# Routed blocks of a mixture-of-experts layer: register reads moved to the head of a step, TensorE's loop turned by one product

## What is computed

```python
shared_out = _silu_and_mul(xf @ shared_w1.T) @ shared_w2.T
probs = jax.nn.softmax(logits.astype(jnp.float32), axis=-1)
routing_weights, selected = jax.lax.top_k(probs, TOP_K)          # 6 of 16
combine = zeros.at[jnp.arange(T)[:, None], selected].add(routing_weights)
gate_up = jnp.einsum('th,eoh->teo', xf, w1)                       # 512 -> 2 * 352
act = _silu_and_mul(gate_up)
moe_out = jnp.einsum('te,tei,ehi->th', combine, act, w2)          # 352 -> 512
```

## Time and profile before

| | us |
|---|---|
| median of 3 runs | 2193.07 |
| lowest and highest run | 2185.72, 2206.43 |
| the profiled execution, its own time | 2193.82 |
| its span, first to last instruction | 2192.1 |
| TensorE busy in the span | 2042.5 (93%) |
| VectorE, ScalarE, GpSimd busy | 1085.6, 949.4, 1039.2 |
| TensorE's granted clock over the span | 0.975 of full speed |

### The profile page before, as it was taken

How to read it: one execution, slowest core, us unless ns; L and a number is a source line. 1 busy time by engine, 2 the same in 40 slices (tenths; PEclk the granted TensorE clock), 3 DMA queues, 4 the chain that set the end, 5 groups by cost and what they waited for, 6 DMA issues and landing times.

```text
span 2192.1 us, 41896 instructions
## 1 busy us (share of the span) xinstructions
PE 2042.5 (93%) x12188; PEld 1828.2 (83%) x12189; DVE 1085.6 (50%) x2355; ACT 949.4 (43%) x2127; POOL 1039.2 (47%) x1070
## 2 busy tenths in 40 slices
PE   3999999999999999999968997899999999999997
PEld 2888888888888888888857886889999999988886
DVE  5555545555667676767545546333333333332322
ACT  4555545554565565656534410233333333333322
POOL 3444434442444445454546206367643223588864
PEclk9999999999999999999878998999999999999999
DMA  8877767777777776756324226467544333489898
GB/s 311 291 247 250 245 227 242 257 240 278 270 260 260 291 266 238 275 205 231 113 84 166 87 86 218 153 215 252 198 139 143 119 118 120 153 201 201 191 189 211
DMA packets 189240, 451.53 MB, mean 206 GB/s; under 512 B 21696, under 2 KB 21952, under 8 KB 189120
## 3 DMA queue, kind: packets, MB, share of 16 engines
q1 hardware_dynamic: 135648, 339.73, 45.3%
q0 software_dynamic: 21504, 51.13, 9.9%
q10 hardware_dynamic: 31968, 59.12, 8.4%
HBM read 276.41 MB, written 173.48 MB: 205 GB/s over the span
## 4 chain that ended last, share of the span: by engine, by line
PE 81%; issue 4%; DMA 3%; DVE 3%; ACT 3%; POOL 3%; SPq 0%; ACTq 0%; POOLq 0%
PE bank L1170 19%; PE bank L1046 13%; PE bank L1180 10%; PE bank L1094 8%; PE bank L1064 6%; PE bank L178 5%; PE bank L730 5%; PE bank L1112 3%; PE bank L740 3%; PE bank L1076 3%; PE bank L747 2%; POOL ex L1353 1%; PE bank L1104 1%; PE bank L478 1%; DMA xT<-xT_ffn 1%
## 5 line engine op out<-in xcount | busy, mean ns | idle before, releaser
L1170 PE MATMUL bank<-w_hi,xT 128*128 x1776 | 477.4, 331 | 19.3 <-issue 17.5
L1046 PE MATMUL bank<-w_hi,xT 128*128 128x512 f32 x1024 | 355.9, 409 | 13.8 <-DMA xT<-xT_att 9.3
L1170 PEld LDWEIGHTS bank<-w_hi,xT 128*128 128x128 f32 x1776 | 316.0, 188 | 42.2 <-issue 40.3
L1339 POOL TENSOR_TENSOR rr<-rr,expo 128x4 f32<-128x4 f32 x128 | 128.9, 1007 | 417.7 <-DVE rr L1456 417.7
L757 DVE TENSOR_TENSOR hT<-bank,hT 128x384 fp32r<-128x384 f32 x143 | 79.7, 557 | 439.2 <-ACT hT L754 439.2
L1170 PE MATMUL bank<-w_lo,xT 128*128 x888 | 286.6, 323 | 0.0
L1046 PEld LDWEIGHTS bank<-w_hi,xT 128*128 128x128 f32 x1024 | 197.8, 193 | 55.3 <-issue 13.2
L1180 PE MATMUL bank<-w_hi,hT 128*128 x666 | 229.5, 398 | 2.1 <-DVE hT L757 2.1
L754 ACT ACTIVATE hT<-bank 128x384 fp32r<-128x384 f32 x143 | 70.2, 491 | 341.8 <-PE bank L747 341.4
L1064 PE MATMUL bank<-w_hi,xT 128*128 128x256 f32 x1024 | 213.6, 292 | 0.0
L1094 PE MATMUL bank<-w_hi,oT 128*128 128x512 f32 x512 | 193.5, 419 | 20.0 <-DVE qkT L1451 18.3
(11 more groups left out here) (228 smaller groups left out, 4535.8 us busy)
## 6 DMA issues: line engine op xcount, KB each, us to landing
xT<-xT_att SPq DMA_DIRECT2D x128, 512.0 KB, 4.1
w_hi<-w_split SPq DMA_DIRECT2D x64, 512.0 KB, 6.6
w_lo<-w_split SPq DMA_DIRECT2D x64, 512.0 KB, 7.4
xg<-blank SPq DMA_DIRECT2D x111, 264.0 KB, 4.4
yg<-blank SPq DMA_DIRECT2D x111, 256.0 KB, 4.6
raw<-in_weights SPq DMA_DIRECT2D x88, 272.0 KB, 3.0
w_split<-w_hi SPq DMA_DIRECT2D x64, 272.0 KB, 3.4
w_split<-w_lo SPq DMA_DIRECT2D x64, 272.0 KB, 3.4
```

Source lines behind the costliest of these rows:

```text
L1046: last = pe.matmul(bank[par][:, :], xT[:, par, a, c * P:(c + 1) * P], w_hl[w][:, fw, c * 512:(c + 1) * 512], start=n == 0, stop=n == 11)
L1170: last = pe.matmul(out_[:, 0:I], xT[:, par, a, c * P:(c + 1) * P], flat(w_hl[w])[:, bass.ds(at + (c * 2 * I + half_ * I), I)], start=n == ...
L1339: pool.tensor_tensor(rr[:, :], rr[:, :], expo[:, :], ALU.pow).then_inc(pw_done, 1)
```

## The change

Three things change, all in the routed blocks. On TensorE a step now begins with all its reads, `w_at` of block i, `w_need` of block i, and `w_at` of block i-2, and then does the second product of block i-2 before the gate half of block i. The last product of the old step i-1 has become the first of the new step i, and the loop has its own shape (`blocks`) with one more step at the end; the order of all products and transpositions is as before. On ScalarE a step begins with the reads of `r_need` and `w_col`. From step ROUNDS_BY = 57 on, ScalarE doesn't read `r_need` but waits for all 6 rounds by a constant; its loop is split in two there. No other engine's program changes.

```diff
--- before.py
+++ after.py
@@ -916,6 +916,7 @@
             step(NBLK - 1, 0, True, False, False, True)
             step(NBLK, 1, False, False, False, True)
 
+        ROUNDS_BY = 3 * B + 9
         ROUTE_AT = 20
         COUNT_AT = 21
 
@@ -1183,15 +1184,21 @@
                             n += 1
                     last.then_inc(yF_done, 1)
 
-                def block_step(i, par, front, nxt, load, back):
+                def block_step(i, par, front, nxt, mid, back):
                     if front:
                         at = pe.value_load(w_at[0:1, bass.ds(i, 1)], min_val=0, max_val=WCOLS)
                         need = pe.value_load(w_need[0:1, bass.ds(i, 1)], min_val=HB, max_val=E * HB)
+                    if back:
+                        last_at = pe.value_load(w_at[0:1, bass.ds(i - 2, 1)], min_val=0, max_val=WCOLS)
+                        pe.wait_ge(hT_hi, NSH + i - 1)
+                        pe.wait_ge(hT_lo, NSH + i - 1)
+                        second_at(last_at, YF[par])
+                    if front:
                         pe.wait_ge(w_ready, need)
                         pe.wait_ge(xs_hi, i + 1)
                         pe.wait_ge(xs_lo, i + 1)
                         first_at(par, at, 0, GATE[par], g_done)
-                    if back:
+                    if mid:
                         pe.wait_ge(hid_done, NSH + i)
                         hidden_transposes(pe, HT_)
                     if nxt:
@@ -1199,17 +1206,23 @@
                         transposed(1 - par, trS)
                     if front:
                         first_at(par, at, 1, UP[par], u_done)
-                    if back:
-                        last_at = pe.value_load(w_at[0:1, bass.ds(i - 1, 1)], min_val=0, max_val=WCOLS)
-                        pe.wait_ge(hT_hi, NSH + i)
-                        pe.wait_ge(hT_lo, NSH + i)
-                        second_at(last_at, YF[1 - par])
+
+                def blocks(step):
+
+                    step(0, 0, True, True, False, False)
+                    step(1, 1, True, True, True, False)
+                    with pe.Fori(2, NBLK - 2, 2) as i:
+                        step(i, 0, True, True, True, True)
+                        step(pe.snap(i + 1), 1, True, True, True, True)
+                    step(NBLK - 1, 0, True, False, True, True)
+                    step(NBLK, 1, False, False, True, True)
+                    step(NBLK + 1, 0, False, False, False, True)
 
                 pe.wait_ge(table_out, 3)
                 pe.wait_ge(added, NSH)
                 pe.wait_ge(x_in[0], 16)
                 transposed(0, trS)
-                sparse(pe, block_step)
+                blocks(block_step)
 
             @block.scalar
             def _(act):
@@ -1289,18 +1302,26 @@
                         act.activation(pr[:, :, :], lg[:, :, :], ACT.Exp).then_inc(ex16, 1)
                 shared(act, shared_step)
 
-                def load(i, par):
-                    need = act.value_load(r_need[0:1, bass.ds(i, 1)], min_val=1, max_val=TOPK)
+                def load(i, par, need):
                     act.wait_ge(rounds, need)
                     act.dma_start(xin[par], xg[bass.ds(i * P, P), :]).then_inc(x_in[par], 16)
 
-                def split_hi(i, par):
+                def rounds_for(i):
+                    return act.value_load(r_need[0:1, bass.ds(i, 1)], min_val=1, max_val=TOPK)
+
+                def weight_at(i):
+                    return act.value_load(w_col[0:1, bass.ds(i, 1)], min_val=D, max_val=DW - 1)
+
+                def split_hi(i, par, col):
                     act.activation(xT[:, par, 0, :], TX_[:, :], ACT.Copy).then_inc(xs_hi, 1)
-                    col = act.value_load(w_col[0:1, bass.ds(i, 1)], min_val=D, max_val=DW - 1)
                     act.activation(cc[:, par:par + 1], xin[par][:, bass.ds(col, 1)], ACT.Copy, scale=0.5)\
                         .then_inc(cc_done, 1)
 
-                def block_step(i, par, front, nxt, load_, back):
+                def block_step(i, par, front, nxt, load_, back, early=True):
+                    if load_:
+                        need = rounds_for(i + 2) if early else TOPK
+                    if nxt:
+                        col = weight_at(i + 1)
                     if back:
                         act.wait_ge(ht_done, NSH + i)
                         hidden_hi(act, HT_)
@@ -1311,10 +1332,10 @@
                     if load_:
                         act.wait_ge(trS, i + 1)
                         act.wait_ge(cc_done, i + 1)
-                        load(i + 2, par)
+                        load(i + 2, par, need)
                     if nxt:
                         act.wait_ge(trS, i + 2)
-                        split_hi(i + 1, 1 - par)
+                        split_hi(i + 1, 1 - par, col)
                     if back:
                         act.wait_ge(yF_done, NSH + i)
                         if not (isinstance(i, int) and i < 3):
@@ -1325,10 +1346,19 @@
                 act.wait_ge(table_out, 5)
                 act.wait_ge(u_done, NSH)
                 for par in range(2):
-                    load(par, par)
+                    load(par, par, rounds_for(par))
+                col = weight_at(0)
                 act.wait_ge(trS, 1)
-                split_hi(0, 0)
-                sparse(act, block_step)
+                split_hi(0, 0, col)
+
+                block_step(0, 0, True, True, True, False)
+                for lo, hi, early in ((1, ROUNDS_BY, True), (ROUNDS_BY, NBLK - 3, False)):
+                    with act.Fori(lo, hi, 2) as i:
+                        block_step(i, 1, True, True, True, True, early)
+                        block_step(act.snap(i + 1), 0, True, True, True, True, early)
+                block_step(NBLK - 2, 1, True, True, False, True)
+                block_step(NBLK - 1, 0, True, False, False, True)
+                block_step(NBLK, 1, False, False, False, True)
 
             @block.gpsimd
             def _(pool):
```

## The result

| | before | after |
|---|---|---|
| median | 2194.89 us | 2242.36 us |
| lowest and highest run | 2185.72, 2206.43 | 2237.61, 2255.67 |
| the profiled execution | 2193.82 | 2255.67 |
| ratio of the times | | 1.022 [1.018, 1.027] |

The change makes the kernel 2.2% slower, 47 us. The forecast was 2238 us, slower with a chance of 0.73. The profiled execution of after is 13 us over the median. About that much lies ahead of the routed blocks (the first second product starts at 1431.4, before at 1417.9) and has nothing to do with the change: in a second profile of after it starts at 1418.3, and that execution took 2249.21.

What follows compares the result with a forecast made beforehand. TensorE bounds the kernel (81% of the chain), and its sequencer's lead decides. 2193.8 + 18 (quiet) + 14 (late) + 12 (scatter) = 2238 us, 2.0% slower; range 2190 to 2275.

Steps and rivals of the forecast that it cites:

- The lead of 2.5 us, not more: Ahead of the second product, TensorE's sequencer arrives 2.5 us early, at most about 34 instructions ahead, whatever it is spared earlier.
- Rival A: TensorE's lead grows by 2 us or more, nearly all of the 32 us comes back: 2168 us; chance 0.10.
- A read costs its duration plus 0.45, the last 0.6: TensorE's register reads: three in a row ahead of the second product take the sum of their durations plus 1.5 us.
- rival B: TensorE's lead grows a little, to 3.0 to 3.3 us, or reads in a row overlap: 2185 to 2205 us; chance 0.17.
- The quiet pair, 0.78 us: Quiet stretch between GpSimd's scattering and gathering: two steps stand still 0.55 us, 0.78 with starts; 24.5 pairs give +18 us net.
- The late term, +14: Last stretch, 35 steps while GpSimd gathers: TensorE's exposed reads +10, shorter leads +8, less some 4 from ScalarE: +14 us.
- S: Sum of the durations of TensorE's three reads in a step; 1.67 us forecast for the late stretch.
- The 8 us for steps without the full lead: Late stretch: in perhaps nine steps the sequencer is 0.9 us short of its 2.5 us lead, +8 us.
- The scatter term, +12: First stretch, 25 steps while GpSimd scatters: standstills of 16 us less 4.8 lost already, +12 us (from 8 to 20).
- ScalarE's head at nothing: ScalarE's reads at step start: before step 57 the copy is 0.35 to 0.65 us late, still covered, so no cost.
- Rival C: ScalarE's head becomes the bound; before step 57 standstill grows 0.4 us in 55 steps: 2260 us; chance 0.13.
- ScalarE's gift late: Late stretch: ScalarE issues row loads a read earlier, giving back TensorE's waits for rows, some 4 us in both buffers.

## Why the prediction came out right, step by step

- **The lead of 2.5 us, not more.** Right, and it carried the sign. With two reads spared behind the second product the first read of a quiet step still starts 2.2 us (with the loop's turn ahead of it) or 2.5 us (without) before the array runs dry. The address operations of the up half are held longer than before (1.5 us apart). Rival A is out. Behind it stood the count of 34 queued instructions against the Trainium skill's 64 (TensorE: Matmul & The Clock Gate, the table at its head): the lead agrees with the first. The queue itself wasn't tested by a run of its own.
- **A read costs its duration plus 0.45, the last 0.6.** Right in the quiet stretch (0.76 apart at 0.30, and 0.6 to 0.7 behind the last). Reads in a row don't overlap, so rival B is out too.
- **The quiet pair, 0.78 us.** Measured, from the starts of second products, 7.24 + 6.91 - 13.40 = 0.75 in the pair shown, and 19.6 / 24.5 = 0.80 on the mean. The shares differ: by the chain 0.28 of standstill and 0.26 of start cost in the step with the turn, none and 0.21 in the other, where I had 0.55 (or 0.58) and 0.15 for each start. Standstills are shorter and starts dearer, which cancels; that the sum agrees so closely is luck. The 0.15 was too little for the rows that it was read from (2.31 against 2.10), and the product of 2.31 in the earlier trace rows follows the up half without a gap in the chain, so that a standstill of the array isn't needed for it.
- **The late term, +14.** Too small: +19.5, and +24.9 in the second profile of the same kernel. S was 1.72 on the mean (forecast 1.67). Standstill and starts were to be 35 x (0.87 + 0.15) + 8 = 44 us; measured are 31.5 put down to issue and 35 starts at some 0.23, together 39.5. Three steps failed. The 4 us for rows were booked twice: they were part of the 26 us that I had already taken off, so my own numbers gave 18. The 8 us for steps without the full lead came to about 2.5: in only five of the 35 steps did the first read start over 0.25 us later than in a quiet step of its kind. And a cost was missing, the clock, 5.8 us here (below). With it the parts make 45.3 of the 45.5 us measured.
- **The scatter term, +12.** Right, from a guess between the two other stretches.
- **ScalarE's head at nothing.** Right for this kernel (with the old ScalarE the quiet stretch is 18.9, with the new 19.6 and 19.5), but for a narrower reason than the one given. I asked whether the low half reaches the array in time, and it does. It must also reach the sequencer in time, if reads follow the second product; in the changed kernel none does. With two behind, the same head costs 5 to 8 us. Rival C didn't come true: nothing is put down to the low half in the quiet stretch, and the loss of a step is the same before and after step 57.
- **ScalarE's gift late.** The waits for rows are gone in the changed kernel, but not by ScalarE's part alone: with the old ScalarE and the changed TensorE they are down to 0.7 us of the array's time as well. ScalarE's part alone left 20.0 us against 26.0, though on another chip. Of these 6 us the array's waits for rows are about 1 (2.2 before, 1.3 with it, both from second product 74 to 109); its waits for issue ahead of the gate half fell from 15.5 to 8.0. Why they did stays open, so the mechanism of this term isn't shown.

## What the runs showed of the chip

**The clock falls after long standstills.** The forecast took all products at full speed, since before had a granted clock of 1.00 throughout. Windows of after around its longest standstill (columns as in the earlier trace rows), then the chain there:

```profile
2205.00:2214.00 9.00, 8.09 (x48) 7.13 (x46) 2.44 (x6) 2.56 (x7) 7.48 (x6) 1.00 1.07 261
2214.00:2217.00 3.00, 0.05 (x2) 0.02 (x1) 1.54 (x3) 0.00 (x0) 2.39 (x3) 0.86 1.10 272
2217.00:2222.00 5.00, 5.00 (x13) 4.14 (x14) 0.00 (x0) 0.60 (x1) 4.17 (x3) 0.50 1.09 280
```

```profile
2214.04 2.95 issue
2216.98 4.20 PE bank L1181 x9
2221.19 2.80 PE bank L1171 x12
...
2226.66 2.26 issue
2228.92 3.48 PE bank L1181 x9
2232.40 2.36 PE bank L1171 x12
```

After 2.95 us of standstill the granted clock was 0.50, that is 1.2 GHz, for some 5 us; the second product took 4.20 instead of 2.36 and the gate half 2.80 instead of 1.93. With the next standstill that is 4.3 us, and with an earlier one (1.81 us at 2165.4, then 3.27 and 2.55 for the two groups) 5.8 in all. In the second profile of the same kernel six standstills did it, two of them these:

```profile
2012.65 2.09 issue
2014.73 3.88 PE bank L1181 x9
...
2023.30 1.83 issue
2025.13 3.91 PE bank L1181 x9
```

In before standstills of 2.41 and 2.53 didn't lower it. In the late stretches of the two profiles of after 13 standstills ahead of the second product lasted 1.8 us or more; nine were followed by a granted clock of 0.50, four (of 1.86 to 2.25 us) weren't. So a standstill of about 2 us can cost another 1.5 to 2.7 us, not each time; what decides it these runs don't tell. The cost is 9.2 us in the second profile against 5.8, which is 3.4 of the 5.4 us by which their late stretches differ.

**The sequencer has work of its own.** Before, TensorE was busy all of the quiet stretch, yet two more reads a step, in either place tried, lengthened it by 18.5 and 21.2 us. Without its pauses its sequencer had been at 5.8 of 6.70 us, 87%, which the page doesn't show.

**Some chips stall.** On two of the chips four steps in the scatter stretch took 8 to 16 us more each, in all five kernels profiled there; their idle time was put down to different releasers, and it stays open.

## What to carry to other kernels

Ask of each register read which compute it hides behind. Ahead of an instruction group it has only the engine's queue, about 2.5 us of TensorE's small products here, and only two reads of 0.75 us fit; behind a group it has the group's own 2.1 us. Split the reads over both, and take away those whose value a register can hold: the two together, not the earlier place, made the kernel 1% faster. Check a copy's due time against the moment at which the sequencer wants it, not the array. Sum the sequencer's own work of a loop body against its period before adding to it, and count a standstill of 2 us on TensorE as worth more than its length.
